# Weight scales from squares on ScalarE, and idle products on TensorE around the attention stage

## What is computed

```python
diffs   = x[:, 1:] - x[:, :-1]                     # up to 8 past differences per token
normed  = diffs / |diffs|
weights = pos_weight * tanh(2 * |diffs|)
g       = softmax(2 * cos(normed, guidance)) @ guidance
traj    = sum(weights * (0.6 * normed + 0.4 * g)) / sum(weights)
x       = layernorm(x + traj)
p       = softmax(x @ Wr + br);  e = argmax(p)     # router, top 1
xn      = layernorm(x) * ln_g + ln_b
y       = (relu(xn @ W1[e] + b1[e]) @ W2[e] + b2[e]) * p[e]
out     = layernorm(x + y)
```

## Time and profile before

| | us |
|---|---|
| median of 3 runs | 217.99 (217.01 to 218.57) |
| the profiled execution, device time | 218.13 |
| its span, first to last instruction | 216.3 |
| busy in the span: DVE, PE, ACT, POOL | 171.1, 150.0, 141.6, 122.3 |
| mean granted TensorE clock over the span | 0.811 of full speed |
| attention stage ends, first block of rows is loaded | about 123 |

### The profile page before, as it was taken

How to read it: one execution, slowest core, us unless ns; L and a number is a source line. 1 busy time by engine, 2 the same in 40 slices (tenths; PEclk the granted TensorE clock), 3 DMA queues, 4 the chain that set the end, 5 groups by cost and what they waited for, 6 DMA issues and landing times.

```text
span 216.3 us, 5485 instructions
## 1 busy us (share of the span) xinstructions
PE 150.0 (69%) x1395; PEld 125.7 (58%) x1395; DVE 171.1 (79%) x792; ACT 141.6 (65%) x425; POOL 122.3 (57%) x210
## 2 busy tenths in 40 slices
PE   0057974998777898674510069999899999899600
PEld 0015753685756487573400059899798898788400
DVE  2447789878998988986868517999999999999910
ACT  2357627483835567737712078999999999998530
POOL 4322213423728775877877240377777787678670
PEclk9999997575888597855555558999999999999955
DMA  5996770000100100001015140222222222220000
GB/s 147 355 364 193 213 200 0 3 0 2 39 13 22 34 25 25 27 28 50 25 52 150 36 89 16 50 66 60 70 74 77 71 64 70 75 64 23 31 10 2
DMA packets 16417, 15.76 MB, mean 73 GB/s; under 512 B 2810, under 2 KB 13142, under 8 KB 16386
## 3 DMA queue, kind: packets, MB, share of 16 engines
q1 hardware_dynamic: 13458, 10.83, 18.3%
q0 software_dynamic: 2272, 4.27, 6.0%
q10 hardware_dynamic: 656, 0.30, 0.5%
HBM read 10.52 MB, written 5.33 MB: 73 GB/s over the span
## 4 chain that ended last, share of the span: by engine, by line
PE 21%; ACT 20%; POOL 18%; DVE 15%; issue 13%; DMA 5%; DVEq 2%; SPq 1%; ACTq 1%; POOLq 1%
POOL rows L357 12%; ACT OUT L672 4%; PE bank L433 3%; PE bank L540 3%; DMA XN<-in_attn_embeddings 3%; ACT xs L649 3%; DVE hl L986 3%; ACT xt L654 3%; PE bank L454 3%; POOL rstd L345 2%; POOL R L349 2%; ACT sq L559 2%; ACT hh L663 2%; PE bank L526 2%; PE bank L528 2%
## 5 line engine op out<-in xcount | busy, mean ns | idle before, releaser
L388 POOL DMA_INDIRECT out<-OUT,tok x39 | 40.4, 1037 | 25.1 <-issue 23.9
L357 POOL DMA_INDIRECT rows<-R,place x32 | 34.0, 1061 | 9.0 <-issue 9.0
L526 PE MATMUL bank<-sel,bias 96*128 96x128 bf16 x156 | 35.2, 226 | 0.0
L540 PE MATMUL bank<-W2hl,hh 128*128 x156 | 32.6, 274 | 3.5 <-issue 2.6
L528 PE MATMUL bank<-xh,W1h 128*128 128x128 f16 x156 | 34.9, 224 | 0.0
L530 PE MATMUL bank<-xh,W1l 128*128 128x128 f16 x156 | 34.7, 223 | 0.0
L529 PE MATMUL bank<-xl,W1h 128*128 128x128 f16 x156 | 34.7, 222 | 0.0
L433 PEld LDWEIGHTS bank<-V,C 128*128 128x128 f32 x128 | 24.9, 299 | 11.2 <-issue 11.2
L986 DVE SCALAR_TENSOR_TENSOR hl<-bank,hh 128x512 f16<-128x512 f32 x39 | 26.9, 690 | 3.0 <-ACT hh L663 2.8
L433 PE MATMUL bank<-V,C 128*128 128x129 f32 x128 | 26.8, 393 | 3.0 <-DVE Y L753 3.0
L543 PE MATMUL bank<-W2hl,hl 128*128 x156 | 27.9, 219 | 0.0
(11 more groups left out here) (161 smaller groups left out, 448.9 us busy)
## 6 DMA issues: line engine op xcount, KB each, us to landing
XR<-rows SPq DMA_DIRECT2D x39, 66.0 KB, 2.0
W<-in_ffn_W SPq DMA_DIRECT2D x1, 2048.0 KB, 11.3
X<-in_attn_embeddings SPq DMA_DIRECT2D x2, 512.0 KB, 9.0
X<-in_attn_embeddings SPq DMA_DIRECT2D x1, 768.0 KB
out<-OUT,tok POOLq DMA_INDIRECT x39
XN<-in_attn_embeddings SPq DMA_DIRECT2D x2, 256.0 KB, 8.2
rows<-R,place POOLq DMA_INDIRECT x32, 2.4
C<-in_constants SPq DMA_DIRECT2D x1, 428.0 KB, 5.2
```

Of the source, the lines that this page charges most:

```text
L357: pool.indirect_dma_start(out=rows[:, :], out_offset=bass.IndirectOffsetOnAxis(ap=place[u % 4][:, k:k + 1], axis=0), in_=R[u % 4][:, k, :] ...
L388: pool.indirect_dma_start(out=out[:, :], out_offset=bass.IndirectOffsetOnAxis(ap=tok[k][:, 0:1], axis=0), in_=OUT[k][:, :], in_offset=None ...
L526: pe.matmul(h, bias3[:, c * P:(c + 1) * P], sel, start=True, stop=False)
L540: pe.matmul(y[:, 0:2 * D], hh[k][:, c * P:(c + 1) * P], w, start=c == 0, stop=False)
```

## The change

- DVE's maxima and the transposition of them in iteration 5 go. ACT sums the squares of W1 and W2 instead: `squares`, one ACTIVATE with accumulation over a piece of 128 x 1024, followed by a drain; two pieces in each of iterations 1 to 4, W1 first, placed between the nT copy and ET. In iteration 3 bias and gains come ahead of them (`squares_bias`).
- PE adds them over the partitions in one product with ones in iteration 4, after a small multiplication by the gains on DVE (`gain_sums`). POOL takes one more power of -0.5 (`weight_roots`) in iteration 5. The `scales` steps are now eleven: 0 to 3 in iteration 5, 4 to 10 in iteration 6.
- PE gets `spin(ps, n)`: n products of bf16 ones, 128x128 by 512 columns, into a PSUM bank whose content nobody needs then; nobody reads them. Four stand ahead of each `nT_` from tile 1 on, one ahead of each of the four products of `logits`, five at the head of iterations 8 to 10, six in place of `infl` in iterations 8 and 9, and 16, 18 and 10 around the waits for `table` and `split_lo`.
- `nT_` waits for N only behind its spins. `logits` waits for the ET of the tile before, since its spins write the bank of sims.
- The two loads of the gains signal a semaphore of their own; the order of the queue is the same.

```diff
-        mx = sb("mx", [P, 16])
-        mx4 = sb("mx4", [4, 8])
+        sums = sb("sums", [P, 16])
+        junk = sb("junk", [P, 2 * FF], BF16)
+        norms = sb("norms", [P, 8])
+        roots = sb("roots", [P, 12])
...
+        sums_ps = bank[7][:, 320:336]
...
-            sp.dma_start(gb[:, 0:1], ln_g.rearrange("(d a) -> d a", a=1)).then_inc(ld["small"], 16)
-            sp.dma_start(gb[:, 1:2], ln_b.rearrange("(d a) -> d a", a=1)).then_inc(ld["small"], 16)
+            sp.dma_start(gb[:, 0:1], ln_g.rearrange("(d a) -> d a", a=1)).then_inc(ld["gb"], 16)
+            sp.dma_start(gb[:, 1:2], ln_b.rearrange("(d a) -> d a", a=1)).then_inc(ld["gb"], 16)
...
+            def weight_roots():
+                pool.wait_ge(s["roots_in"], 1)
+                pool.tensor_tensor(roots[:, 0:4], norms[:, 0:4], half[:, :], ALU.pow).then_inc(s["roots"], 1)
...
+                if i == 5:
+                    weight_roots()
...
+            def spin(ps, n):
+                for _ in range(n):
+                    pe.matmul(ps, ones16[:, :], ones16[:, :].unsqueeze(1).to_broadcast([P, 4, P]), start=True, stop=True)
...
             def nT_(u):
-                pe.wait_ge(s["n"], u + 1)
                 if u >= 1:
                     pe.wait_ge(s["nT_sb"], u)
+                    spin(nT_ps[:, :], 4)
+                pe.wait_ge(s["n"], u + 1)
...
-                    pe.wait_ge(ld["small"], 64)
+                    pe.wait_ge(ld["small"], 32)
                 if u >= 1:
                     pe.wait_ge(s["shifted"], u)
+                if u == 2:
+                    pe.wait_ge(s["sums_read"], 1)
+                pe.wait_ge(s["ET"], min(u + 3, NU))
                 for k in range(NT):
+                    spin(sims_ps[:, :], 1)
...
             for i in range(0, NU + 3):
-                if i == 5:
-                    pe.wait_ge(s["maxima"], 1)
-                    pe.wait_ge(s["xT_sb"], 3)
-                    pe.transpose(xT_ps[0:4, 0:P], mx[:, 0:4], ident).then_inc(s["maxT_ps"], 1)
+                if i == NU:
+                    pe.wait_ge(s["nT_sb"], NU)
+                if i >= NU:
+                    spin(nT_ps[:, :], 5)
                 if i < NU:
                     nT_(i)
                 if i >= 3:
                     logits(i - 3)
                 if i < NU:
                     sims(i)
-                if i == 5:
-                    pe.wait_ge(s["max4"], 1)
-                    pe.matmul(xT_ps[:, P:P + 4], ones[0:4, :], mx4[:, 0:4], start=True, stop=True).then_inc(s["maxb_ps"], 1)
                 if 1 <= i <= NU:
                     traj(i - 1)
                 if i >= 3:
                     rank(i - 3)
+                if i == 4:
+                    pe.wait_ge(s["sums"], 6)
+                    pe.wait_ge(s["gains"], 1)
+                    pe.wait_ge(s["shifted"], 2)
+                    pe.matmul(sums_ps, ones[:, :], sums[:, :], start=True, stop=True).then_inc(s["sums_ps"], 1)
                 if i < NU:
                     infl(i)
+                elif i < NU + 2:
+                    spin(nT_ps[:, :], 6)
                 if 2 <= i <= NU + 1:
                     xT_(i - 2)
             pe.wait_ge(s["counted"], NU)
             pe.matmul(log_ps[:, 300:300 + E], ones16[:, :], carry16[:, :], start=True, stop=True).then_inc(s["tot_ps"], 1)
+            spin(nT_ps[:, :], 16)
             pe.wait_ge(s["table"], 1)
+            spin(nT_ps[:, :], 18)
             pe.wait_ge(s["split_lo"], 1)
+            spin(nT_ps[:, :], 10)
...
+            def squares(w, q):
+                if q == 0:
+                    act.wait_ge(ld["w1" if w is W1 else "w2"], 16)
+                act.activation(junk[:, :], w[:, 2 * q:2 * q + 2], ACT.Square, accum_out=sums[:, (8 if w is W1 else 4) + q:(9 if w is W1 else 5) + q])
+                act.drain()
+                if q % 2:
+                    act.nop().then_inc(s["sums"], 1)
+            def squares_bias():
+                act.wait_ge(ld["bias"], 96)
+                act.wait_ge(ld["gb"], 32)
+                act.activation(junk[0:96, 0:FF], bias[:, 0:FF], ACT.Square, accum_out=sums[0:96, 12:13])
+                act.drain()
+                act.nop().then_inc(s["sums"], 1)
+                act.activation(sums[:, 13:15], gb[:, :], ACT.Square).then_inc(s["sums"], 1)
...
+                if 1 <= i < 3:
+                    squares(W1, 2 * i - 2)
+                    squares(W1, 2 * i - 1)
+                if 3 <= i < 5:
+                    if i == 3:
+                        squares_bias()
+                    squares(W2, 2 * i - 6)
+                    squares(W2, 2 * i - 5)
...
+            def gain_sums():
+                dve.wait_ge(s["sums"], 4)
+                ts(sums[:, 0:4], sums[:, 8:12], sums[:, 13:14], None, ALU.mult).then_inc(s["gains"], 1)
...
             def scales(step):
-                v = scl[:, 8:12]
+                n, q = norms, roots
+                col = lambda tile, c: tile[:, c:c + 1]
                 if step == 0:
-                    power(scl[:, 0:1], v[:, 0:1], 5, False)
-                    power(scl[:, 2:3], v[:, 2:3], 8, False)
+                    dve.wait_ge(s["sums_ps"], 1)
+                    dve.tensor_reduce(n[:, 1:4], sums_ps[:, 0:12].rearrange("p (g k) -> p g k", g=3), AX.X, ALU.add)
+                    dve.tensor_copy(n[:, 5:8], sums_ps[:, 12:15]).then_inc(s["sums_read"], 1)
                 elif step == 1:
-                    power(scl[:, 0:1], v[:, 0:1], 5, True)
-                    power(scl[:, 2:3], v[:, 2:3], 8, True)
+                    stt(col(n, 0), col(n, 6), 132.0, col(n, 7), ALU.mult, ALU.add)
+                    stt(col(n, 4), col(n, 3), col(n, 7), col(n, 5), ALU.mult, ALU.add)
                 elif step == 2:
-                    tt(scl[:, 12:13], v[:, 3:4], scl[:, 0:1], ALU.mult)
-                    ts(scl[:, 13:14], v[:, 1:2], 0.5, None, ALU.mult)
+                    stt(col(n, 1), col(n, 1), 128.0, col(n, 4), ALU.mult, ALU.add)
                 elif step == 3:
-                    stt(scl[:, 14:15], scl[:, 12:13], 2.0 ** -13, scl[:, 13:14], ALU.mult, ALU.max)
+                    ts(n[:, 0:4], n[:, 0:4], 2.0 ** -60, None, ALU.max).then_inc(s["roots_in"], 1)
                 elif step == 4:
-                    power(scl[:, 1:2], scl[:, 14:15], 0, False)
+                    dve.wait_ge(s["roots"], 1)
+                    ts(q[:, 0:4].bitcast(I32), q[:, 0:4].bitcast(I32), POW2_MASK, None, ALU.bitwise_and)
                 elif step == 5:
-                    power(scl[:, 1:2], scl[:, 14:15], 0, True)
+                    ts(col(q, INVX).bitcast(I32), col(q, QX).bitcast(I32), -1.0, float(254 << 23), ALU.mult, ALU.add)
+                    ts(col(q, SCL1 + 1), col(q, Q1), 2.0 ** 15, None, ALU.mult)
+                    ts(col(scl, 0), col(q, QX), 2.0 ** 10, None, ALU.mult)
+                    ts(col(scl, 2), col(q, Q2), 2.0 ** 15, None, ALU.mult)
                 elif step == 6:
-                    tt(scl[:, 4:5], scl[:, 0:1], scl[:, 1:2], ALU.mult)
+                    stt(col(q, SCL1), col(q, QH), 2.0 ** 5, col(q, INVX), ALU.mult, ALU.mult)
                     ts(gbs[:, :], gb[:, :], scl[:, 0:1], None, ALU.mult)
                 elif step == 7:
+                    tt(scl[:, 1:2], col(q, SCL1), col(q, SCL1 + 1), ALU.min)
+                elif step == 8:
+                    tt(scl[:, 4:5], scl[:, 0:1], scl[:, 1:2], ALU.mult)
+                elif step == 9:
                     tt(scl[:, 5:6], scl[:, 4:5], scl[:, 2:3], ALU.mult)
                     ts(bias[:, 0:FF], bias[:, 0:FF], scl[0:96, 4:5], None, ALU.mult)
-                elif step == 8:
-                    power(scl[:, 3:4], scl[:, 5:6], 0, False)
-                    ts(bias[:, FF:FF + D], bias[:, FF:FF + D], scl[0:96, 5:6], None, ALU.mult)
-                elif step == 9:
-                    power(scl[:, 3:4], scl[:, 5:6], 0, True).then_inc(s["scales_w"], 1)
+                elif step == 10:
+                    ts(scl[:, 3:4].bitcast(I32), scl[:, 5:6].bitcast(I32), -1.0, float(254 << 23), ALU.mult, ALU.add)
+                    ts(bias[:, FF:FF + D], bias[:, FF:FF + D], scl[0:96, 5:6], None, ALU.mult).then_inc(s["scales_w"], 1)
...
             for i in range(-2, NU + 4):
-                if i == 5:
-                    dve.wait_ge(s["maxT_ps"], 1)
-                    dve.tensor_reduce(mx4[:, 4:5], xT_ps[0:4, 0:P], AX.X, ALU.max)
-                    dve.drain()
-                    ts(mx4[:, 0:4], ident[0:4, 0:4], mx4[:, 4:5], None, ALU.mult).then_inc(s["max4"], 1)
+                if i == 4:
+                    gain_sums()
                 if i >= 1:
                     window(i)
                 if i + 2 < NU:
...
                     guide()
                 if i >= -1:
                     factors(i)
-                if 2 <= i < 5:
-                    maxima2(i - 2)
-                if i == 4:
-                    maxima2(3)
-                if i == 5:
-                    dve.wait_ge(s["maxb_ps"], 1)
```

(14 more changed lines are left out.)

51 lines of the change are left out of this document (16 added, 35 removed).

## The result

The changed kernel takes 210.13 us in the median of 4 runs (209.85 to 211.09), the kernel before 218.28 (217.01 to 218.71) beside it: the ratio is 0.9644, with an interval of 0.9591 to 0.9696. The profiled execution took 209.85 us with a span of 207.7, against a span of 216.3.

What follows compares the result with a forecast made beforehand. The prediction took POOL's roots, waiting for DVE's variances, to bound the kernel. Terms of 2.5 (stage), 0.1 (last transpose) and 1.0 (table) made 3.6 us: 218.1 - 3.6 = 214.5 us, range 211.5 to 219.5.

Steps and rivals of the forecast that it cites:

- What bounds the kernel.: Attention stage: POOL's roots wait for DVE's variances; bringing the last root forward from 101.60 us brings the expert stage equally forward.
- So inside the loop an upper clock only pays for its own spins ... and nothing is won there.: Loop over ACT, PE and DVE: logits with spins take 1.96 us at the upper clock against 1.88 at the lower.
- the sum: Whole kernel: 2.5 us from the stage, 0.1 from a shorter last transpose, 1.0 at the table; 3.6 us won, 214.5.
- rival C: Spins fail to hold the clock in logits; three of six loops low cost 1.65 us more each: 219.5 us, chance 0.18.
- DVE runs as before: After iterations 5 and 6: DVE unchanged, so 2.5 us carry to the last root and through the twelve scatters.
- The remaining loop read as 10.0 us.: Distance between `x1c` at 67.14 and 77.14, logits 1.88 us included, taken as what remains when the maxima are gone.
- Spins' price.: Spins on PE, eight added per iteration: 0.225 us each at the upper clock and 0.43 at the lower.
- The head, 1.5 us late.: Iteration 1: spins ahead of nT(1) and a pair of squares delay the first `x1c` from 33.38 to 34.9 us.
- ACT as the bound in iterations 3 and 4.: From the first `x1c` ACT sets the pace: 10.75 us with bias and gains, then 9.7; lg comes 2.1 us earlier.
- rival B: ACT eats the gain: a square costs 1.6 us, head late by 2.6; 2.3 us less won, 216.8 us, chance 0.24.
- rival D: More than forecast: head not late (1.5 us) and iteration 5 makes up another 1.5; 211.5 us, chance 0.10.
- Table.: Spins around the table wait: ACT waits less for the first h products, between 0.4 and 1.4 us won, 1.0 taken.

Runs made afterwards that it cites:

- third chip: Chip of the third group: the changed kernel unchanged, 212.59 us (0.9679 of before), beside versions with 28 more spins or without spins ahead of nT(1) and nT(2).
- kernel with early spins: Changed kernel plus 28 spins before and in the first tile's work: 208.98 us on one chip, 212.21 us (0.9657 of before) on a later one.
- fourth group: Repetition on a fourth chip in more rounds: changed kernel unchanged, 215.2 us (0.9805 of before); the same with 28 more spins in the head, 212.21 us.
- second group: Runs on another chip with the changed kernel unchanged as base, 212.16 us; beside it that kernel without logits' spins, 216.8 us, and without nT's, 216.12 us.

## Why the prediction failed where it did

**What bounds the kernel.** Right: the last root moved from 101.60 to 94.08, and the end followed it, 113.6 us behind it for 114.7. That the 3.6 us of iteration 4 were on the path is right as well: with spins in both kernels, 13.2 us with them and 9.4 without.

**"So inside the loop an upper clock only pays for its own spins ... and nothing is won there."** This is the step that failed in the loop, where 2.4 us of the sum were missed; the other 2.6 are in the head, below. It counted logits alone. Correlations (1.97 to 1.07), trajectory products (3.81 to 2.05) and in some rounds the influence sums (2.08 to 1.16) get shorter too, and stand in one queue ahead of what DVE waits for. The busy time by stretch in the earlier trace rows had said so: PE 9.35 of 10.0 us at the lower clock. The row was used for rival C and not for the forecast. Without maxima the clock is worth 5.4 us of the loop (68.4 to 63.0), or 2.6 against the other profile without spins (65.6). With the maxima still there it is worth 1.7 (69.4 to 67.8); that the slow rounds of PE lie under DVE's there fits the 13.2 us above and is not shown for the others. The sum came as near as it did because two errors offset each other: it had the loop 4.0 us shorter by DVE's relief alone and by 0 through the clock, and the runs give 1.0 and 5.4.

**Where in the loop.** The sum had the seven distances at 10.75, 9.7, 9.85, 9.4 and then 8.6, 9.3 and 7.8 as before. Measured against it, the two held to be ACT's are 0.5 us shorter each, the third 0.4 shorter, the fourth 0.3 longer, and the last three 1.2 shorter in all. Of these last the sum said "DVE runs as before"; the fifth (8.6 before, 7.9 after) and the seventh (7.8, 7.3) got shorter with the spins and the maxima still there as well (8.0 and 7.3).

**The remaining loop read as 10.0 us.** The links of the earlier trace rows were taken as what is left without maxima, logits at 1.88 us included. They were a round at the lower clock. At the upper one PE's spins and logits take 1.57 us from the first spin to the last product (65.53 to 67.10), not 1.96: the f32 products go in between spins at 0.35 us for each pair.

**Spins' price.** Right: four take 1.89 us in the first round at the lower clock and 1.04 at the upper one as durations, ten in a row 2.33 us with 0.38 for the last one, so 0.22 apart; 0.225 was taken. The Trainium skill, in TensorE: Matmul & The Clock Gate, gives 215.7 ns from start to start for 512 columns in its section "Wait — 56ns, not 53.3ns?" and the trace agrees. The 131 ns that the Trainium skill gives in the section Back-to-back issue gap of the same page the trace does not bear out.

**The head, 1.5 us late.** Wrong in this profile: 1.1 us early against before, 2.6 against the sum, and so the larger part of the miss. The timeline of the head, answering to the earlier trace rows:

```profile
18.34 1.89 PE L410 MATMUL bank<-ones 128*128 128x512 bf16 x4
...
21.12 0.60 ACT L604 ACTIVATE nT<-bank 128x512 f32<-128x512 f32 x1 [1.57 <-PE bank L438]
21.61 1.05 ACT L635 ACTIVATE junk<-W 128x1024 bf16<-128x1024 f32 x1
21.77 1.07 PE L472 MATMUL bank<-nT,gdT 128*64 128x512 f32 x2 [0.69 <-ACT nT L604]
...
22.77 2.05 PE L447 MATMUL bank<-V,C 128*128 128x129 f32 x16
22.82 1.06 ACT L635 ACTIVATE junk<-W 128x1024 bf16<-128x1024 f32 x1
...
24.07 0.59 ACT L610 ACTIVATE ET<-bank 64x512 f32<-64x512 f32 x1
...
24.75 1.16 PE L421 MATMUL bank<-gdz,ET 64*128 64x129 f32 x8
```

The nT copy moved by 1.2 us where 1.8 were forecast, ET(1) came at 24.07 instead of 24.95. But correlations and trajectory products then ran at 2.4 GHz, and the influence sums start at 24.75, before their old 25.83. I had the clock rise as before or later, not earlier. Other profiles of the same head have the first `x1c` at 33.0, 34.3, 35.0, 35.2 and 35.7: the forecast of 34.9 describes four of them and not this one. The term has no fixed value, and should have stood in the range with both signs; the early side of it was missing. On the third chip the profiled execution had its `x1c` at 35.0 and took 212.76 us, inside the range, with the loop just as short. That the first measurement fell outside is thus in part chance, and one that fell inside would not have made the step about the loop right.

**ACT as the bound in iterations 3 and 4.** Nearly, but too large. Squares start 1.21 us apart (21.61, 22.82), not 1.3; no run shows the 1.6 of rival B. The sum of 10.75 and 9.7 us added durations as they stand, though successive activations overlap by about 0.1 us. From one x1 to the next ACT took 10.20 and 9.24 us, of which it stood idle 0.43 and 0.47, so its work was 9.8 and 8.8. DVE, which waits for nothing in the second of these, is the bound there, and x1 starts 0.23 us behind `x1c`; ACT is less than 0.5 us from being it. The x1 starts forecast at 45.8, 55.5 and 65.3 came at 42.72, 51.96 and 61.39. Rival B, in which ACT eats the gain, has no ground left; rival D, 211.5, was the nearest, right in that the head is not late, though iteration 5 made up 0.4 us and not 1.5.

**Rival C.** The clock stayed up from 38.5 to 96.5 us. It is the kernels with one place of the stage's spins taken away that show how near it was.

**Table.** Right as a sum, 1.1 us, and partly by luck. The table's spins make 0.7, and ACT's waits for the first h products, which run at 1.00, fell by as much (1.4 to 0.7). The stage's spins make another 0.9 behind the last root (114.5 to 113.6 with the table's spins, 115.2 to 114.3 without), and 0.5 is lost again by the other half of the change (114.7 before, 115.2 without spins); neither was in the sum.

## What to carry to other kernels

When an engine whose clock varies is nearly full at the lower one, price the clock over everything in its queue ahead of the next consumer, not over the one product that is named in the chain. Price two reliefs of one loop together, since each alone may only uncover the other. A product whose only use is to keep the clock up belongs also into the head, before the first products that are waited for. And one profile is not enough to put down a difference of 1% to an edit: the same code had heads of 32.3 to 35.7 us, and the same loop without spins took 68.4 us in one profile and 65.6 in another.

## What the runs showed of the hardware

The same kernel has two levels on one chip: 209.63 us once and 212.46 to 212.76 three times, with spans of 207.7 and 210.4 to 210.7. The two profiles at hand, at 209.85 and 212.76, differ by 2.7 us in when the first `x1c` comes, and that by whether the clock was up before or during the second tile's products. The Trainium skill says in TensorE: Matmul & The Clock Gate, section "What's actually happening", that the point of the rise varies from run to run of one kernel; these profiles, though of two chips, agree. The kernel with early spins still has two levels (207.15 and 207.45, 210.52 and 210.74), and what its second is was not profiled.

Chips differ by more than the time of the kernel before tells. That is 218.2 to 218.9 us everywhere, but the kernel after gained 8.2 us at first, 6.0 in the third group, and in the fourth only 3.4. The span of its profile there is 5.5 us above the first one: 3.4 us are in the head, 1.9 in the loop, 0.2 in the rest. The part in the loop is idle time of DVE ahead of `lg`, in the fourth and the fifth distance. The timeline of the fourth group's profile for the first of these, and that of the first profile for the same iteration:

```profile
70.31 0.28 PE L463 MATMUL bank<-Wr,xT 128*128 128x8 f32 x2
71.65 0.19 DVE L826 TENSOR_TENSOR lg<-bank,brb 128x32 f32<-128x32 f32 x1 [0.68 <-PE bank L463]
```

```profile
66.82 0.28 PE L463 MATMUL bank<-Wr,xT 128*128 128x8 f32 x2
67.40 0.17 DVE L826 TENSOR_TENSOR lg<-bank,brb 128x32 f32<-128x32 f32 x1
```

The profile puts the 0.68 us down to PE, but the last product of logits had ended 1.06 us before. In the fifth distance it is 0.92 us, with the product done 1.44 before. The second group's profile of this kernel has the same two (0.53 and 0.77), and the early-spin kernel on the fourth chip too (0.69 and 0.92); the first profile and the third group's have neither. Behind its last root the early-spin kernel has two more on the fourth chip, of 1.0 and 1.3 us, marked "issue", and takes 116.3 us there instead of 113.8. What DVE waits for isn't settled; no view here shows it. The mark "issue" alone is no sign of such a gap: waits of 1.03, 0.85 and 0.5 us carry it in the profiles of the second and fourth group, and stand at the same places and as long in the first profile and the third group's, with a releaser named.
